# Feed-forward stage: the bf16 cast of the turned keys is moved from DVE into ACT's queue, behind the two query copies

## The reference

```python
x = x + 0.5 * _L0_ffn_ref(_layernorm(x), ...)
x = x + _L0_attn_ref(_layernorm(x), ...)
x = x + 0.5 * _L0_ffn_ref(_layernorm(x), ...)
x = x + 0.5 * _L1_ffn_ref(_layernorm(x), ...)
x = x + _L1_attn_ref(_layernorm(x), ...)
x = x + 0.5 * _L1_ffn_ref(_layernorm(x), ...)
```

```python
qkv = shift_token(x) @ wqkv
q, k = l2norm(q) * qs, l2norm(k) * ksc
q, k = rotary_xpos(q, k)
o = local_attention(q, k, v)           # windows of 64, each with the window before it
x = x + o @ wo
h = layernorm(shift_token(x)) * lg + lb
a, g = split(h @ w1 + b1)
x = x + (a * gelu(g)) @ w2 + b2
```

## Time and profile before

| what | us |
|---|---|
| median of 3 runs (lowest, highest) | 2481.72 (2479.73, 2485.17) |
| the profiled execution, its own time | 2473.8 |
| its span, first to last instruction | 2471.8 |
| what lies around the span | 2.0 |

### The profile page before, as it was taken

One profiled execution on the slowest core, in us unless ns is written; L12 is line 12 of the kernel. 1 busy time (PEld: TensorE's weight loads), 2 busy tenths in 40 slices (PEclk: granted clock), 3 DMA queues, 4 the chain that ended last, 5 costly groups with the idle time before them and its releaser, 6 DMA issues. The chain is left out here.

```text
span 2471.8 us, 54760 instructions
## 1 busy us (share of the span) xinstructions
PE 2194.1 (89%) x22630; PEld 1635.5 (66%) x22630; DVE 1708.8 (69%) x2815; ACT 1466.5 (59%) x2389; POOL 1096.0 (44%) x800
## 2 busy tenths in 40 slices
PE   2799999999999869999969999999999997697968
PEld 1567767777777656666636666677777774495758
DVE  3677777878878546777737777778888884563556
ACT  0476767667676515556546667677677674363634
POOL 4655555656556110000026565656556550550245
PEclk8799999999999969999979999999999998698979
DMA  7000000069999970000000000000000003121122
GB/s 154 1 2 1 2 2 1 1 78 124 131 146 148 147 85 1 2 2 2 2 1 1 2 2 2 1 2 2 1 2 2 2 1 78 52 66 36 35 75 79
DMA packets 211370, 91.01 MB, mean 37 GB/s; under 512 B 79700, under 2 KB 206721, under 8 KB 210996
## 3 DMA queue, kind: packets, MB, share of 16 engines
q1 hardware_dynamic: 202596, 72.27, 21.8%
q0 software_dynamic: 6080, 11.76, 1.5%
q10 hardware_dynamic: 2448, 3.48, 0.7%
HBM read 24.51 MB, written 63.41 MB: 36 GB/s over the span
## 5 line engine op out<-in xcount | busy, mean ns | idle before, releaser
L485 POOL TENSOR_TENSOR work<-work,rot_tables 128x512 f32<-128x512 f32 x256 | 448.2, 1771 | 423.8 <-ACT work L589 423.8
L493 POOL TENSOR_TENSOR work<-work 128x1024 f32<-128x1024 f32 x128 | 303.5, 2371 | 11.2 <-DVE work L919 1.2
L919 DVE TENSOR_TENSOR work<-work,rot_tables 128x1024 f32<-128x1024 f32 x128 | 164.9, 1288 | 124.9 <-ACT work L589 124.9
L1076 DVE TENSOR_REDUCE small<-psum 128x4 f32<-128x1024 f32 x128 | 156.6, 1224 | 94.7 <-PE psum L1595 94.6
L1318 PE MATMUL psum<-qkv_w_hi,h_hi 128*128 128x512 f32 x384 | 184.5, 481 | 41.4 <-POOL h_lo L512 39.1
L1475 PE MATMUL psum<-centered,ffn_w 128*128 128x256 f32 x768 | 191.4, 401 | 6.1 <-DVE centered L980 2.9
L936 DVE TENSOR_TENSOR work<-work,small 128x1024 f32<-128x1024 f32 x128 | 160.3, 1254 | 48.9 <-ACT small L603 47.0
L700 ACT ACTIVATE work<-psum 128x1024 f32<-128x1024 f32 x128 | 131.2, 1025 | 101.1 <-PE psum L1602 101.1
L1413 PE MATMUL psum<-work 64*128 64x128 f32 (+1 forms) x2048 | 178.9, 304 | 0.0
L500 POOL TENSOR_TENSOR y_all<-centered,squared 64x256 f32<-64x256 f32 x64 | 48.6, 760 | 290.6 <-ACT squared L649 288.1
L1475 PEld LDWEIGHTS psum<-centered,ffn_w 128*128 128x128 f32 x768 | 146.3, 197 | 36.5 <-DVE centered L980 17.7
(11 more groups left out here) (283 smaller groups left out, 5530.3 us busy)
## 6 DMA issues: line engine op xcount, KB each, us to landing
h_area<-mean_weights SPq DMA_DIRECT2D x24, 2048.0 KB, 24.8
tile_x<-h_area SPq DMA_DIRECT2D x39, 128.5 KB, 2.1
stage<-in_consts ACTq DMA_DIRECT2D x1, 3009.0 KB, 12.4
tile_x<-h_area SPq DMA_DIRECT2D x39, 64.5 KB, 1.8
work<-in_x SPq DMA_DIRECT2D x4, 512.0 KB, 27.6
expert_w<-in_ew SPq DMA_DIRECT2D x1, 2048.0 KB, 8.5
expert_w<-in_ew SPq DMA_DIRECT2D x8, 256.0 KB, 6.8
work<-y_tokens SPq DMA_DIRECT2D x4, 512.0 KB, 6.0
```

What stands on the lines that cost most here:

```text
L485: last = pool.tensor_tensor(b[:, :, :, o_], a[:, :, :, i_], tab[:, l, 1, t, :, o_].unsqueeze(2).to_broadcast([P, 2, HEADS, 32]), ALU.mult)
L493: pool.tensor_tensor(rC[:, t, :], rC[:, t, :], rB[:, t, :], ALU.add).then_inc(f_sum, 1)
L919: dve.tensor_tensor(g(rC[:, t, :]), g(rA[:, t, :]), tab[:, l, 0, t, :, :].unsqueeze(2).to_broadcast([P, 2, HEADS, DH]), ALU.mult)\
L1076: dve.tensor_reduce(dst, PS[:, 0:2, :].rearrange("p b (t j) -> p b t j", t=TILES), AX, ALU.max, negate=True).then_inc(a_smax, 1)
```

## The change

`copy_q` on ACT gets a third instruction: after the two query copies it waits for `f_kb` and casts `kT` (SBUF, f32) to `kT_bf` (bf16). `f_qsb` is now set by that cast. `k_out` on DVE keeps the copy out of PSUM, which sets `f_kb` by itself; its wait on the chain semaphore and its cast are gone. PE's `scores` has the same waits as before.

```diff
@@ ACT, copy_q(i)
                     act.wait_ge(f_qT, i + 1)
                     q = by_half(PS[:, 3:5, :])
                     act.activation(in_halves(qT), q, ACT.Copy)
-                    act.activation(in_halves(qb[:, :, :]), q, ACT.Copy).then_inc(f_qsb, 1)
+                    act.activation(in_halves(qb[:, :, :]), q, ACT.Copy)
+                    act.wait_ge(f_kb, i + 1)
+                    act.activation(kb[:, :, :], kT, ACT.Copy).then_inc(f_qsb, 1)
@@ DVE, k_out(i)
                     dve.wait_ge(f_kT, i + 1)
-                    link(dve.tensor_copy(in_halves(kT), by_half(PS[:, 5:7, :])))
-                    dve.tensor_copy(kb[:, :, :], kT).then_inc(f_kb, 1)
+                    dve.tensor_copy(in_halves(kT), by_half(PS[:, 5:7, :])).then_inc(f_kb, 1)
```

## The result

The changed kernel takes 2512.51 us (median of 4 runs, 2508.21 to 2515.66), the kernel before 2480.72 (4 runs, 2479.19 to 2485.17): 31.8 us more, ratio 1.0129 with a 95% interval of 1.0105 to 1.0154. The forecast was 2515.0, that is 33.3 more. A second measurement of the same kernel, on another chip, gave 2513.85 us where the kernel before took 2487.2: 26.7 us more, ratio 1.0101 (1.0079 to 1.0123, so 20 to 31 us).

The account below looks back on a forecast made before the run. The prediction took the end of ACT's L589 to hold each layer-1 turn, though PE looked busiest. 30.4 (layer-1 turns) + 1 (layer-0 turns) + 1.9 (last turns) = 33.3 us on 2481.7 gave 2515.0 us, range 2503 to 2527.

Parts of the forecast that it names:

- Which instruction holds the turn: In 32 layer-1 turns L589 waits for ACT itself; DVE's cosines and PE's masks start from its end.
- The pitch: ACT's cast makes the next instruction start 0.95 us later (0.90 to 1.06); 30.4 us over 32 layer-1 turns.
- The wait for `f_kb`: ACT's added wait before its cast: DVE's copy has ended 0.85 us early, so it costs 0.
- The masks: PE's mask matmuls in layer-1 turns wait some 0.9 us longer, for the end of L589.
- The layer-0 turns: 28 turns with the norm: L589's idle time covers the cast; 0.03 us each, 1 us in sum, 0 to 4.
- the rival in which all turns pay: Layer-0 turns not covered, costing 0.95 us each: 2541 us in all; chance 0.06.
- The edges: Last turn of each pass: PE's masks wait 0.95 us longer, for the cast; 1.9 us for two, first turn 0.
- Clock: PE's new idle time is 4% of a turn; no loss of granted clock expected from 1.00.
- The sum: Over the whole kernel 30.4 + 1 + 1.9 = 33.3 us more, giving 2515.0 us, 1.3% more; chance 0.78.

Follow-up runs that it names:

- experiment 1: Kernel before, DVE's cast kept, ACT doing the same cast once more into a tile nothing reads: 2509.9 us, ratio 1.0144.
- experiment 2: Kernel before without the cast of the keys on any engine, except for the first item of each pass: 2483.18 us, ratio 1.0015.
- Experiment 3: Changed kernel with ACT's cast moved one place back, behind L589 instead of ahead of it: 2510.31 us, ratio 1.0137 against the kernel before.
- Experiment 5: Changed kernel with ACT's cast done twice, first into a tile nothing reads: 2568.26 us, ratio 1.0323 against the kernel before.
- the mirror: Kernel before, ACT copying the queries once and DVE casting them to bf16: 2479.74 us, ratio 0.9994; measured again 2477.72 us, ratio 0.9967.
- experiment 6: The changed kernel measured again, nothing altered: 2513.85 us, ratio 1.0101 against the kernel before.

## Why the prediction was right

- *Which instruction holds the turn.* L589 with no idle time before it was the row on which all rested. Experiments 1 and 2 confirm it from both sides: adding the cast to ACT alone gives the whole loss, removing it from DVE alone gives nothing. Experiment 3 adds what the prediction did not say: the scores need the cast keys hardly later than L589 ends, so in this turn two paths are tight and not one.
- *The pitch.* 0.95 us was taken from PSUM copies plus 0.04; the trace has 0.95 (487.03 to 487.98). A layer-1 turn grew by 0.93 us, so 32 x 0.93 = 29.8 us against a forecast of 30.4.
- *The wait for `f_kb`.* Costed at 0, and it is 0: L612's group has 0.0 us of idle time before it.
- *The masks.* Their matmuls have 0.67 us of idle time ended by L589, where I had forecast 0.9. They start 3.94 us after L609 instead of 3.11 (489.15 - 485.21, before 483.37 - 480.26), 0.83 later.
- *The layer-0 turns.* Forecast 0.03 us each, 1 us in sum. From 110.03 to 433.24 before and from 113.27 to 437.23 after, 13 turns grew by 0.75 us, 0.058 each; all 28 together grew by 1.5. Experiment 5 shows that this was cover and not indifference; the rival in which all turns pay would have been right with one cast more.
- *The edges.* Forecast 1.9 us for the last turns of the two passes. The masks of the last turn start 2.98 us after L609 (which starts at 2081.05) where it was 2.04 (after 2040.35) in the second pass, 0.94 later; in the first pass it is 3.93 where it was 2.88, 1.05 later. That makes 2.0 us. PE in the second pass, before and after:

```profile
2042.39 1.24 PE L1377 MATMUL psum<-masks_bf,eye_bf 128*128 128x512 bf16 x6 [0.15 <-issue]
2084.03 1.24 PE L1378 MATMUL psum<-masks_bf,eye_bf 128*128 128x512 bf16 x6 [1.10 <-issue]
```

- *Clock.* The granted clock stayed at 1.00 in both stretches.
- *The sum.* 29.8 + 1.5 + 2.0 = 33.3 us by the turns, the very sum of the forecast. The medians differ by less: 31.8 us in the first measurement, 26.7 in the second and 28.9 in experiment 1. The interval of the second ends at 31. That the first came within 1.5 us of the forecast is in part luck, since what lies outside the turns varies by more than that between executions of one kernel: between the passes, the two profiles of the mirror have 463.38 and 458.78 us. Whether something outside the turns gives a few us back stays open.

What the sum did not contain is in the profiled execution, whose span grew by 40.9 us (2471.8 to 2512.7) and not by 33. Taken apart by the starts of L609: some 32 us are turns and edges; 3.3 us lie in the first turn of the first pass (27.22 us from L609 to L609, before 23.87); 2.7 in the last one (27.06, where its neighbours have 24.37; the granted clock was 0.66 from 830 to 834 us there); 2.8 between the last L609 of the first pass and the first of the second. The first is no part of the change: that turn takes 25.57 us in experiment 2, with nothing added on ACT, and 23.63 in experiment 1, with the cast added. The second did not come back in experiment 6 (24.36). The third is told below.

## What to carry to other kernels

A share of busy time says which engine has room on average, and an instruction lands in one place of a queue. Before moving work to the less busy engine, look at what stands behind the new place: if the next instruction there has no idle time before it and two engines wait for its end, the whole pitch of the moved instruction is paid in every turn, while the engine it left only waits longer. Where the next instruction does have idle time, that time is the cover, with the 0.1 us by which two instructions of ACT overlap here added to it, and what goes beyond is paid in full. A second path that needs the moved result (here the scores) can be as tight as the first; look at both before choosing the place.

## What the runs showed of the hardware

**The 2.8 us between the passes.** Counted from the last L609 of the first pass, ACT in the changed kernel is 0.65 us later than before in the middle of `attn()` (a copy at 1064.13, before 1041.78) and 3.85 us later at its end (1289.04, before 1263.49). In the kernel before, PE's granted clock is 1.00 from 1246.5 to 1252.5 us; at about the same place of the changed kernel, 1268.0 to 1274.4, it is 0.51, near the lower of its two levels (1.2 GHz, against 2.4). In both kernels PE had waited 1.21 us for a copy of ACT just before, and waits another 1.11. The same sixteen matmuls, before and after:

```profile
1248.14 1.07 PE L1614 MATMUL psum<-work 128*32 128x256 f32 x16
1271.36 1.94 PE L1615 MATMUL psum<-work 128*32 128x256 f32 x16
```

Why the clock fell there was not tried and stays open. It is no cost of the cast that these runs show: from the last L609 of the first pass to the first of the second the nine profiles have 458.78 to 469.18 us, with 460.55 in experiment 5, where ACT casts twice.

**DVE and POOL side by side.** At the start of a pass PE comes out of a quiet stretch at a granted clock of 0.50, and its matmuls of 512 columns take 0.63 us at first and 0.39 once the clock is 1.00. At the start of the second pass the faster ones begin 7 us after the first of them in the kernel before (1273.1 to 1280.3) and 4 us after it in the changed kernel (1298.7 to 1302.7). So the second half of the projection is ready sooner, and DVE's second cosine product starts before POOL's sum and not after it. DVE, POOL and ACT in the kernel before:

```profile
1281.19 3.09 DVE L919 TENSOR_TENSOR work<-work,rot_tables 128x1024 f32<-128x1024 f32 x1 [1.69 <-ACT work L589]
1280.83 2.37 POOL L493 TENSOR_TENSOR work<-work 128x1024 f32<-128x1024 f32 x1
1292.99 1.02 ACT L609 ACTIVATE work<-psum 128x1024 f32<-128x1024 f32 x1 [3.34 <-PE psum L1327]
```

and in the changed kernel:

```profile
1305.48 1.94 DVE L920 TENSOR_TENSOR work<-work,rot_tables 128x1024 f32<-128x1024 f32 x1 [0.41 <-ACT work L589]
1302.75 3.57 POOL L485 TENSOR_TENSOR work<-work,rot_tables 128x512 f32<-128x512 f32 x2 [4.12 <-ACT work L589]
1306.40 3.21 POOL L493 TENSOR_TENSOR work<-work 128x1024 f32<-128x1024 f32 x1
1318.42 1.02 ACT L609 ACTIVATE work<-psum 128x1024 f32<-128x1024 f32 x1 [5.76 <-PE psum L1328]
```

DVE's product takes 1.23 us when it starts ahead of POOL's (where POOL's L485 starts 0.04 us behind it), and POOL's sum takes 2.37 when it starts first. Whichever starts second waits for the other and is drawn out in the profile. In the kernel before, the 3.09 us end 1.08 us after POOL's sum has ended at 1283.20. In the changed kernel, the 1.94 us end 1.10 us after POOL's L485 has ended at 1306.32, and POOL's 3.21 us end 2.2 us after DVE's product has ended at 1307.42. So the second one does almost all of its work after the first has ended. The Trainium skill says that a DVE operation with two SBUF inputs and a GpSimd operation that reads SBUF lock the port pair that they share, and that the one that comes second fully blocks (SBUF — State Buffer, SBUF: two separate sides); these rows agree.

The change of order costs nothing here. ACT's idle time ahead of the first L609 of a pass is 5.76 us instead of 3.34, but only because ACT's work before it ends sooner, 13.98 us after PE's first matmul of the pass instead of 16.52. Counted from that matmul, the first L609 starts 19.86 us later in the kernel before and 19.73 in the changed one. The nine profiles have 18 starts of a pass: five with 5.76 us (both profiles of the changed kernel and experiment 3 in the second pass, experiment 2 in both), where the faster matmuls begin after 4.4 us and L609 starts after 19.73 to 19.75, and thirteen with 3.33 to 3.35, where they begin after 7.2 us or more and L609 starts after 19.83 to 19.87. Since experiment 2 has the early rise without a cast on ACT and experiment 5 has two casts without it, it does not come from the cast. Why the clock rises earlier in some executions stays open.
